# One stage of a 16-image kernel: its attention front in two parts for two images, its expert rows in one queue of 270 tiles

## The reference, cut to what matters

```python
    t = _to_tokens(x)
    t = t + _L2_attn_ref(_ln_t(t), ...)   # landmark attention
    t = t + _L2_ffn_ref(_ln_t(t), ...)    # GELU experts, 2 of 8 per token
...
    kernel_1 = softmax(q @ k_lm^T * scale); kernel_2 = softmax(q_lm @ k_lm^T * scale); kernel_3 = softmax(q_lm @ k^T * scale)
    kernel_2_inv = _iterative_inv(kernel_2)   # z = 2.0 * z - z @ mat @ z, six times
    out = kernel_1 @ (kernel_2_inv @ (kernel_3 @ v))
...
    gate = softmax(xt @ Wg); topv, topi = top_k(gate, 2); topv = topv / (sum(topv) + 1e-06)
    for e in range(8):
        h = gelu(xt @ W1[e] + b1[e]); ye = h @ W2[e] + b2[e]
        out = out + ye * scores[:, e:e + 1]
```

## Time and profile before

| stretch | us | TensorE busy | VectorE busy | granted TensorE clock |
|---|---|---|---|---|
| whole span | 5302.9 | 89% | 67% | 0.96 |
| front(0) alone | 69.37 | 38.79 us | 30.70 us | 0.68 |
| front(1) and choice(0) | 82.36 | 48.61 us | 49.58 us | 0.69 |
| twelve windows, 2384.59 to 3480.15 | 1095.56 | 964.21 us | 649.23 us | 0.96 |
| last three windows | 292.80 | 260.47 us | 160.55 us | 0.99 |
| dense stage | 1529.95 | 1422.86 us | 1036.84 us | 0.98 |

### The profile page before, as it was taken

One profiled execution on the slowest core, in us unless ns is written; L12 is line 12 of the kernel. 1 busy time (PEld: TensorE's weight loads), 2 busy tenths in 40 slices (PEclk: granted clock), 3 DMA queues, 4 the chain that ended last, 5 costly groups with the idle time before them and its releaser, 6 DMA issues.

```text
span 5302.9 us, 81731 instructions
## 1 busy us (share of the span) xinstructions
PE 4738.9 (89%) x25633; PEld 2629.4 (50%) x25633; DVE 3577.1 (67%) x7651; ACT 2996.8 (57%) x5516; POOL 1023.8 (19%) x1349
## 2 busy tenths in 40 slices
PE   6999999999999969588888888888999999999999
PEld 1222222222222223367777878777655555555554
DVE  6788888888888636556565655655577667667765
ACT  2666667676676724145555555557655554554552
POOL 2222223222232212023333333333100000000000
PEclk7999999999999989689999999999999999999999
DMA  2622223322233112235454554544211111111112
GB/s 61 166 78 69 73 66 98 84 66 77 66 92 83 49 31 28 68 111 169 135 169 138 154 152 145 162 132 134 64 49 52 45 48 51 47 47 51 49 45 76
DMA packets 396856, 461.35 MB, mean 87 GB/s; under 512 B 86136, under 2 KB 248144, under 8 KB 394320
## 3 DMA queue, kind: packets, MB, share of 16 engines
q1 hardware_dynamic: 362688, 409.11, 26.7%
q0 software_dynamic: 20576, 35.55, 2.4%
q10 hardware_dynamic: 13168, 11.48, 0.8%
HBM read 309.59 MB, written 129.84 MB: 83 GB/s over the span
## 4 chain that ended last, share of the span: by engine, by line
PE 34%; DVE 16%; issue 4%; DVEq 4%; ACT 2%; ACTq 0%; SPq 0%; DMA 0%
PE n_ps_f L2212 4%; PE n_ps_f L2205 4%; PE n_ps_xy L1860 4%; PE n_ps_h L1850 3%; PE n_ps_c L2252 3%; PE n_ps_h L2264 2%; PE n_ps_f L2199 2%; PE n_ps_f L1708 2%; DVEq L2084 1%; PE n_ps_xy L2268 1%; PE n_ps_f L1054 1%; DVE n_stats L1030 1%; PE n_ps_h L2268 1%; DVE n_xln L1042 1%; DVE n_down_weights L2083 1%
## 5 line engine op out<-in xcount | busy, mean ns | idle before, releaser
L664 ACT ACTIVATE a_probs<-ps_b 128x512 f32<-128x512 f32 x2048 | 1111.3, 595 | 558.7 <-PE ps_b L748 535.6
L496 DVE TENSOR_REDUCE a_negmax<-ps_a 128x1 f32<-128x1024 f32 x1024 | 1214.5, 1220 | 242.3 <-PE ps_a L696 213.0
L1663 ACT ACTIVATE n_hidden<-n_ps_h,n_b 128x128 f32<-128x128 f32 x1472 | 419.1, 373 | 346.9 <-PE n_ps_h L1850 346.1
L760 PE MATMUL ps_o<-a_probs,a_v_ones 128*32 128x512 f32 x4096 | 547.6, 607 | 0.5 <-ACT a_probs L664 0.5
L1860 PE MATMUL n_ps_xy<-n_down_weights,n_hidden 128*128 x2944 | 411.9, 284 | 79.2 <-ACT n_xy L1677 73.3
L696 PE MATMUL ps_a<-a_k_stack,a_q_stack 96*128 96x512 bf16 x1408 | 404.0, 394 | 58.5 <-DMA a_k_stack<-split_scratch 27.5
L748 PE MATMUL ps_b<-a_q_stack,a_k_stack 99*128 99x512 bf16 x1408 | 442.3, 386 | 14.8 <-ACT a_probs L664 11.9
L1860 PEld LDWEIGHTS n_ps_xy<-n_down_weights,n_hidden 128*128 128x128 f32 x2944 | 370.7, 196 | 117.3 <-issue 113.2
L2149 ACT ACTIVATE n_down_weights<-n_ps_h 128x512 f32<-128x512 f32 x288 | 172.2, 598 | 427.1 <-PE n_ps_h L2264 319.1
L1850 PE MATMUL n_ps_h<-n_xy,n_up_weights 128*128 128x128 f32 x2944 | 403.2, 281 | 3.2 <-issue 1.5
L1368 POOL DMA_INDIRECT rows_scratch<-n_xln,n_index_out x256 | 257.1, 1004 | 666.8 <-DVE n_index_out L1521 563.2
(11 more groups left out here) (349 smaller groups left out, 8154.3 us busy)
## 6 DMA issues: line engine op xcount, KB each, us to landing
n_up_weights<-in_L_ffn_W_dram SPq DMA_DIRECT2D x368, 256.0 KB
n_up_weights<-score_scratch SPq DMA_DIRECT2D x512, 128.0 KB, 2.9
split_scratch<-a_pieces SPq DMA_DIRECT2D x128, 256.0 KB
rows_scratch<-n_zero SPq DMA_DIRECT2D x16, 1472.0 KB, 9.6
outs_scratch<-n_xy SPq DMA_DIRECT2D x176, 128.0 KB
n_xg<-rows_scratch SPq DMA_DIRECT2D x80, 256.0 KB, 3.4
a_q_stack<-split_scratch SPq DMA_DIRECT2D x66, 256.0 KB, 5.0
a_k_stack<-split_scratch SPq DMA_DIRECT2D x66, 256.0 KB, 5.6
```

The lines of the kernel that those rows point to most:

```text
L496: dve.tensor_reduce(negmax[:, b, t:t + 1], bank, axis=AX.X, op=ALU.max, negate=True).then_inc(ring_read, 1)
L664: act.activation(probs[:, m % PROBS, 512 * k:512 * k + 512], ps_b[:, k, :], ACT.Exp).then_inc(b_exp, 1)
L760: last = pe.matmul(ps_o[32 * j:32 * j + 32, 512 * k:512 * k + 512], v_ones[:, t, J * g + j, :], probs[:, (J * quad + j) % PROBS, 512 * k:5 ...
L1663: last = act.activation(hidden[:, j % 2, f, :], ps_h[j % 2][:, 128 * f:128 * f + 128], ACT.Gelu, bias=b1[:, bass.ds(e, 1), f:f + 1].rearra ...
```

## The change

Three things change together.

**Front in two parts.** `front` keeps all that comes ahead of the Newton iteration and the product of the third softmax with v; the iteration, the mixing and the last product are `back`. Window i now holds front(i + 3), back(i + 2) and choice(i + 1), and three windows without expert work come ahead: front(0); front(1) and back(0); front(2), back(1) and choice(0). The Newton steps stand four slots apart from slot 1 on and have a PSUM bank of their own (`pn`); the front turns through three single banks, and most of its operations on 1024 columns become two on 512.

**One queue of full tiles.** An expert's rows run on across images: a tile is closed when it is full, and only the last image of each of two groups (images 0 to 2, images 3 to 15) closes what is open. So there are 16 tiles for each image and 7 more for each group, 270 in all. The windows hold 4, 14, 24, twelve times 16, and 36 tiles (`begun`), and the two halves of a tile are spread evenly over the 46 slots (`steps_of`). `routing` keeps the open tiles and the queue (66 VectorE instructions an image, nine of them on 240 columns of one partition). A tile's place in DRAM is looked up, so SyncE reads a number also ahead of each load of rows and each store, which take one tile each. `clear` goes; eight indirect transfers fill up the open tiles at each of the two closes.

**Combine.** Images 0 to 2 are gathered and combined in windows 5 to 7, images 3 to 15 in the dense stage's windows 0 to 12, from slot 35 on. There the helper that takes the largest experts works on four token tiles at a time (twice 1024 columns in place of once 2048), in buffers that it shares with the second stage.

```diff
-ROWS = 128 * ((2 * N + 8 * 127) // 128)
+EARLY_IMAGES = 3
+EARLY_TILES = 2 * N * EARLY_IMAGES // 128 + 7
...
+    for lo in range(0, NT, tiles):
+        shape = (128, tiles, E, E)
...
-        TILES = (N * K + E * 127) // 128
-        PAIRS = (TILES + 1) // 2
-        GROUPS = (TILES + 3) // 4
+        PER_IMAGE = N * K // 128
+        FLUSHES = (EARLY_IMAGES - 1, B - 1)
+        TILES = PER_IMAGE * B + 2 * (E - 1)
+        PAIRS = TILES // 2
...
+        sure = [0] + [PER_IMAGE * (i + 1) - (8 if i + 1 < EARLY_IMAGES else 0) for i in range(B - 1)] + [TILES]
+        begun = [0] + [sure[i] - AHEAD + (2 if i == 1 else 0) for i in range(1, B)] + [TILES]
...
+        banks, pn = (pa[:, 0:512], pa[:, 512:1024], pb_[:, 0:512]), pb_[:, 512:1024]
+        BY_DVE, BY_ACT = "gate v s2 s1 norm kv".split(), "tok lnt q k s3 k1t e3t".split()
+        units = [(x, k) for x in "gate tok lnt q k v".split() for k in range(HALVES)] + [("s2", 0), ("s1", 0), ("s1", 1), ("s3", 0), ("s3", 1)]
+        units += [("norm", 0), ("k1t", 0), ("k1t", 1), ("e3t", 0), ("e3t", 1), ("kv", 0)]
+        bank_of = {unit: banks[n % 3] for n, unit in enumerate(units)}
...
+            side_by_side([front(1), back(0)])
+            side_by_side([front(2), back(1), choice(0)])
...
-            experts(0, [front(2), choice(1)])
-            for i in range(1, B - 2):
-                experts(i, [front(i + 2), choice(i + 1)])
+            for i in range(B - 3):
+                experts(i, [front(i + 3), back(i + 2), choice(i + 1)])
+            experts(B - 3, [back(B - 1), choice(B - 2)])
             experts(B - 2, [choice(B - 1), dense_attention(0)])
...
+        def steps_of(i, slot):
+
+            steps = 2 * (begun[i + 1] - begun[i])
+            return range(2 * begun[i] + steps * slot // SLOTS, 2 * begun[i] + steps * (slot + 1) // SLOTS)
...
-            def clear(i):
-                sp.dma_start(x_dram[i][:, :].rearrange("(t p) c -> p t c", p=128),
-                             zero[:, :].unsqueeze(1).broadcast_to((128, TILES, C))).then_inc(zeroed, 16)
...
+            def load_rows(q):
+                if q >= 4:
+                    sp.wait_ge(x_ps, q - 3)
+                i = routing_of[2 * q]
+                if 2 * q == sure[i]:
+                    sp.wait_ge(S["owner_up"], i + 1)
+                    sp.wait_ge(scattered, scattered_by(i + 1))
+                for n in range(2):
+                    c = code_of(2 * q + n)
...
+            def store_pair(q):
+                sp.wait_ge(moved, q + 3)
+                for n in range(2):
+                    c = code_of(2 * q + n)
+                    sp.dma_start(tiles_of(y_dram, 2 * q + n)[bass.ds(c, 1), :, :].rearrange("a p c -> (a p) c"), xy[:, q % 2, 256 + 128 * n:384 + 128 * n]).then_inc(y_stored[q % 2], 16)
...
+                pairs = early_pairs if i < EARLY_IMAGES else PAIRS
...
+            for i in range(B):
+                scatter(i)
+                if 0 <= i - GATHER_AFTER < EARLY_IMAGES:
+                    gather(i - GATHER_AFTER)
+            for i in range(EARLY_IMAGES, B):
+                gather(i)
...
+                for k in range(HALVES):
+                    half = slice(512 * k, 512 * k + 512)
+                    dve.wait_ge(*filled(i, "gate", k))
+                    dve.scalar_tensor_tensor(u[:, half], bank_of["gate", k], b3[:, :], u[:, half], ALU.add, ALU.mult).then_inc(S["read_v"], 1)
+                    dve.drain()
+                    dve.tensor_tensor(u[:, half], u[:, half], x1[:, half], ALU.add).then_inc(S["x2_up"], 1)
...
+            def back(i):
+                yield 0
+                m2t, tok_next = m2ts[i % 2], tok_nexts[i % 2]
                 dve.tensor_scalar(z[:, :], m2t[:, :], fro[:, :], None, ALU.mult)
 
                 dve.tensor_scalar(zt[:, :], m2[:, :], fro[:, :], None, ALU.mult).then_inc(S["z0_up"], 1)
-
                 for it in range(NEWTON):
-                    yield 24 + 2 * it
+                    yield 2 + 4 * it
                     dve.drain()
                     dve.wait_ge(mz_ps, i * NEWTON + it + 1)
-                    dve.tensor_copy(mz[:, :], pa[:, 0:128]).then_inc(mz_up, 1)
-                    yield 25 + 2 * it
+                    dve.tensor_copy(mz[:, :], pn[:, 0:128]).then_inc(mz_up, 1)
+                    yield 4 + 4 * it
                     dve.wait_ge(znew_ps, i * NEWTON + it + 1)
...
+                dve.tensor_tensor(need[:, :], left[:, :], counts[:, NT, :], ALU.add)
+                dve.scalar_tensor_tensor(limit[:, :], has[:, :], 128.0, left[:, :], ALU.mult, ALU.subtract)
+                dve.scalar_tensor_tensor(base[:, :], open_id[:, :], 128.0, left[:, :], ALU.mult, ALU.add)
...
+                yield dve.tensor_tensor(marked[:, :, :], places, by_expert(first), ALU.is_equal)
+                dve.tensor_tensor(entered[:, :, :], places, by_expert(first), ALU.is_ge)
+                dve.tensor_tensor(closed[:, :, :], places, by_expert(end), ALU.is_ge)
...
+            run_dense(lambda i: combine(i + EARLY_IMAGES) if i + EARLY_IMAGES < B else None)
...
+                    yield 1 + 4 * it
                     if it == 0:
                         pe.wait_ge(S["z0_up"], i + 1)
                     else:
                         pe.wait_ge(z_up, i * NEWTON + it)
-                    pe.matmul(pa[:, 0:128], m2t[:, :], z[:, :], start=True, stop=True).then_inc(mz_ps, 1)
-                    yield 25 + 2 * it
+                    pe.matmul(pn[:, 0:128], m2t[:, :], z[:, :], start=True, stop=True).then_inc(mz_ps, 1)
+                    yield 3 + 4 * it
                     pe.wait_ge(mz_up, i * NEWTON + it + 1)
-                    pe.matmul(pa[:, 512:640], zt[:, :], mz[:, :], start=True, stop=True)
-                    pe.matmul(pa[:, 640:768], mz[:, :], zt[:, :], start=True, stop=True).then_inc(znew_ps, 1)
...
+            more = beside(i) if beside else None
+            experts_and_stages(i, [choice(i + 1, True), attention(i + 2)] + ([more] if more else []))
```

More of the change, by code:

```diff
@@ new lines, in front @@
+                yield 17
+                for k in range(HALVES):
+                    bank, half = begin("v", k)
+                    for t in range(4):
+                        col = 512 * k + 128 * t
+                        last = pe.matmul(bank[:, 128 * t:128 * t + 128], xt[:, col:col + 128], wqkv[:, 2 * C:3 * C], start=True, stop=True)
+                    last.then_inc(S["front_ps"], 1)
+                yield 19
+                bank, _ = begin("s2")
+                pe.wait_ge(S["lm_up"], i + 1)
@@ new lines, in front @@
+                pe.matmul(bank[:, 0:LM], q_lm[:, :], kt[:, 0:N:STEP], start=True, stop=True).then_inc(S["front_ps"], 1)
+                yield 20
+                for k in range(HALVES):
+                    bank, half = begin("s1", k)
+                    for t in range(4):
+                        col = 512 * k + 128 * t
+                        last = pe.matmul(bank[:, 128 * t:128 * t + 128], qt[:, col:col + 128], k_lm[:, :], start=True, stop=True)
+                    last.then_inc(S["front_ps"], 1)
@@ L1892, in _ @@
             dense_attention, dense_choice, run_dense = dense["tensor"](pe)
[L1893 to L1895 removed]
+            pipeline(pe, (front, back), choice, experts, dense_attention, dense_choice, first_rows)
+            down(TILES - 1)
+            pe.wait_ge(moved, PAIRS + 2)
             run_dense()
```

767 lines of the change are left out of this document (452 added, 315 removed).

## The result

The changed kernel takes 5495.84 us (median of 4 runs, 5489.19 to 5499.75) against 5304.09 for the kernel before (4 runs, 5300.96 to 5309.0): 1.0359 times as long, 95% interval 1.0341 to 1.0377. Forecast were 5188 and a gain of 117 us; it is a loss of 192.

What follows compares the result with a forecast made beforehand. TensorE's amount of work was taken to bound a window, with VectorE close behind. Second stage -143, windows ahead +25, last windows -26 and dense stage +27 gave -117 on 5304.7 us: 5188 us, range 5085 to 5270.

Steps and rivals of the forecast that it cites:

- So TensorE's amount of work bounds a window: Second stage of the kernel before: TensorE busy 80.35 of 91.30 us a window, 2.1 us of it per tile.
- The sum for a steady window: Second stage, windows of 16 tiles: 65.65 + 10.95 + 6.9 - 1.4 - 2.1 = 80.0 us.
- The first three windows: Second stage, windows of 4, 14 and 24 tiles: 76, 80 and 92 us, the first two bound by VectorE's chain.
- The head of a window: Start of a steady window: TensorE idles 9 us behind VectorE's normalisations, in place of 2.1, so +6.9 us.
- VectorE then still waits 12 us: Steady window of 80.0 us: VectorE, with 68 us of work, waits 12 us where it waited 30.
- rival D: Head of a window: VectorE and TensorE stand still in turn, windows of 98 us, total 5422 us; chance 0.12.
- rival C: Steady windows: stalls at the head lower TensorE's clock, 4 us more each, total 5240 us; chance 0.08.
- The windows ahead: Three windows without expert work ahead of window 0: 177 us against 151.7, +25 us.
- The last windows: End of the second stage: 68 tiles for 69 and front(15) moved one window ahead, -26 us.
- The dense stage: Inherits the combine of twelve images, 1.63 us each, and the helper's halves, half a microsecond an image: +27 us.
- B (SyncE): Second stage: SyncE's three address reads per tile bound the long windows, about 72 us more, total 5260 us; chance 0.06.
- E: Dense stage pays all of the combine, 4.7 us each: 5217 to 5231 us; chance 0.61 together with the forecast.

Runs made afterwards that it cites:

- the fill: The changed kernel with 14 to 22 idle matmuls ahead of each of TensorE's four long waits in a window: 5449.85 us.
- the moves: The changed kernel with the choice's normalisation a window earlier, tiles ahead of TensorE's waits, routing spread out, dense combine over slots 14 to 44: 5301.8 us.
- tiles in bursts: The changed kernel with more tiles in the slots just ahead of TensorE's four long waits and fewer in the others: 5389.34 us.
- first experiment: The kernel before with 16 of the 23 tiles of each image, its front, choice and routing unchanged: 5279.04 us against 5301.21.

## Why the prediction was wrong

**The step that failed is the first:** "So TensorE's amount of work bounds a window". It was read from a busy share of 88% and from TensorE's waits, which were short. They were short because tiles filled the time that VectorE took: without seven of them the waits for the gate and the copies grew from 4.2 us a window, (25.3 + 24.9) / 12 in the earlier trace rows, to 10.2, (75.9 + 56.8) / 13, and the old window is 1.3 us shorter, not 14.7. The sum for a steady window took 65.65 us of TensorE's work and 14.35 of idle time; the trace has 73.6 and 25.4. The work itself was sized about right: at a clock of 0.95 it is 63.2. So 11 of the 19 missing us are idle time, and 8 are the same work at a lower clock. The thing to add up was the path that runs through both lists in turn: the same instructions in other slots made the window 10.0 us shorter. The first three windows missed by 11 to 17 us as well: 92.0, 96.6 and 102.9 for 76, 80 and 92.

**The head of a window** was walked rightly: 9 us of idle time were booked, 3 and 6, and the trace has 4.4 and 5.1. That the longest waits would stand in the first fifth was wrong: of the four, only the shortest ends there, 11 us behind the window's start, the next 26 us behind it, and the two longest 70 and 82. **The middle was not walked.** The routing's 40 further instructions were counted into VectorE's 68 us, which came out (99.0 less some 32 of waits is 67), but not as a piece ahead of what TensorE needs. There 6.8 and 5.5 us were lost, 12.3 a window.

**"VectorE then still waits 12 us"** failed: some 32 remain. The iteration's round trips still hold 12.8 of them, (26.8 + 11.5) / 3, and the end of the window about as much again, (15.1 + 7.5 + 12.7) / 3: for work that stands elsewhere in the list these waits were no reserve. "It keeps every wait" stood in the text as the upper bound, 98 us a window; the measured 99.0 is that bound, and rival D, which had 0.12, is the theory that held, though it named the head alone. Its total of 5422 fell short by 74, as the windows ahead, the last windows and the dense stage cost more too.

**The clock (rival C)** was right as an effect and was priced at 4 us a window; the fill shows at least 3.4. It came on top of D, where the prediction held the two as alternatives. The Trainium skill's rule in "TensorE: Matmul & The Clock Gate", section "HAM oscillation", that a loop which idles for its data loses the clock each time round, agrees with the trace here: 0.50 behind the waits shown above, 0.83 in windows with 25 us of idle time, 0.94 after the moves had cut that to 14.

**The windows ahead:** 185.3 for 177, a term of the right kind, 8 us too small. **The last windows** gained nothing, where 26 were counted: windows 12 to 15 take 393.7 us, before 292.8 and one of 91.6.

**The dense stage** was mis-sized: +27 forecast, +65.5 measured. The halves cost 1.40 us a window instead of 0.5. A combine with its gathers costs 3.28 instead of 1.63, a price that came from one interval between two stores (3845.82 to 3948.11), where intervals without a combine differ by nearly as much among themselves, from 100.3 to 101.8. That interval holds the whole combine of the kernel before, from the first to the last of its 16 instructions:

```profile
3850.24 0.61 DVE L1585 SCALAR_TENSOR_TENSOR maps<-n_rows,n_weight,maps 128x128 f32<-128x128 f32 x2
...
3869.93 0.61 DVE L1585 SCALAR_TENSOR_TENSOR maps<-n_rows,n_weight,maps 128x128 f32<-128x128 f32 x2
```

In both kernels TensorE waits 2.1 us for VectorE there, and a second time at the next product. This second wait and the matmuls behind it, first in the kernel before, then in the changed one:

```profile
3873.26 1.99 PE L2252 MATMUL n_ps_c<-n_xg,n_xt 128*128 128x512 f32 x2 [0.40 <-DVE n_xg L2090]
3875.09 1.02 PE L2264 MATMUL n_ps_h<-n_v,n_small 128*128 128x512 f32 x2
```

```profile
4000.91 2.07 PE L2477 MATMUL n_ps_c<-n_xg,n_xt 128*128 128x512 f32 x2 [1.12 <-DVE n_xg L2315]
4002.78 1.91 PE L2489 MATMUL n_ps_h<-n_v,n_small 128*128 128x512 f32 x2
```

The second wait is 0.7 us longer in the changed kernel, and the clock stays at its lower level for longer: two matmuls take 1.91 us where they took 1.02. What makes that wait longer isn't shown; the gathers, which had ended ahead of the interval in the kernel before, run inside it now, from 4000.87 on.

Of the rest, B (SyncE) didn't come about: in the whole second stage TensorE waits once for weights, 2.9 us, and 4.3 us with tiles in bursts. E counted 4.7 us for a combine, nearer to the measured 3.28 than the forecast's 1.63.

What stays open: how much of the old window's missing gain (first experiment) belongs to the clock, which fell there too, and how much to the order. No run separates them. No run takes the windows ahead or the last windows by themselves.

## What to carry to other kernels

A busy share of 88% doesn't make an engine the bound where two lists in fixed order feed each other: take some of its work out and see whether the time follows, or walk the path through both lists over the whole period before pricing the work removed. A wait of the other engine is a reserve only where work can be put into it: the same instructions in other slots were worth 16 us of 99 here. A price read from a single interval is to be held against the scatter of the intervals beside it: 1.63 us stood against a scatter of 1.5, and the same work cost twice as much in other surroundings.

## What was not expected of the hardware

Work taken from TensorE came back as clock: with 7 of 23 tiles gone its busy time fell by 7.1 us a window where the tiles were 14.7, at 0.86 for 0.96. And idle matmuls in its waits made a kernel faster, by 46 us, with nothing else changed but two waits for the banks that they write.
